# A mixture-of-experts stage cut into tiles of 256 slots instead of 512

## The reference

```python
x = x + _L0_gnn_ref(_layernorm(x), ...)        # 6 steps of a graph network on 3125 nodes, D = 256
x = x + _L0_ffn_ref(_layernorm(x)[None], ...)[0]

def _L0_ffn_ref(x, Wg, bg, bias, W1, b1, W2, b2):   # 8 experts, top 2, 256 -> 512 -> 256, float32
    gate_logits = x_flat @ Wg + bg + bias
    topk_vals, topk_idx = jax.lax.top_k(gate_logits, TOP_K)
    topk_w = jax.nn.softmax(topk_vals, axis=-1)
    h = jax.nn.relu(jnp.einsum('td,edh->teh', x_flat, W1) + b1)
    y = jnp.einsum('teh,ehd->ted', h, W2) + b2
    out = jnp.einsum('ted,te->td', y, combine)
```

## Time and profile before

| | |
|---|---|
| median of 3 runs | 2399.18 us |
| the profiled execution | 2399.45 us, its span 2397.7 us |
| mean granted clock of TensorE | 0.933 of 2.4 GHz |
| TensorE busy over the span | 84% |
| VectorE, ScalarE, GpSimd busy | 48%, 23%, 7% |
| expert stage | from 2087.5 us (first load issued) to 2320.4 us (last store landed) |
| tiles in it | 17, from one eviction to the same one of the next tile 12.7 us |

### The profile page before, as it was taken

How to read it: one execution, slowest core, us unless ns; L and a number is a source line. 1 busy time by engine, 2 the same in 40 slices (tenths; PEclk the granted TensorE clock), 3 DMA queues, 4 the chain that set the end, 5 groups by cost and what they waited for, 6 DMA issues and landing times.

```text
span 2397.7 us, 30332 instructions
## 1 busy us (share of the span) xinstructions
PE 2013.7 (84%) x11085; PEld 1418.0 (59%) x11086; DVE 1157.5 (48%) x2353; ACT 545.4 (23%) x1164; POOL 158.5 (7%) x228
## 2 busy tenths in 40 slices
PE   1766669999999999999999999999999952099960
PEld 1522236568756785578556865678567941088850
DVE  7599971345333452445233533444234565166643
ACT  0245541112211121112111221112112213132310
POOL 1011110000000000000000000000000003500026
PEclk7789999999999999999999999999999966599985
DMA  9500000000000000000000000000000114522224
GB/s 292 179 1 0 0 1 1 1 1 1 2 1 1 1 2 1 1 1 1 2 1 1 1 2 1 1 1 2 1 1 1 55 56 146 169 92 78 81 88 134
DMA packets 77945, 83.61 MB, mean 35 GB/s; under 512 B 10236, under 2 KB 72639, under 8 KB 77812
## 3 DMA queue, kind: packets, MB, share of 16 engines
q1 hardware_dynamic: 72244, 68.96, 9.1%
q0 software_dynamic: 5568, 12.82, 1.7%
HBM read 37.94 MB, written 43.81 MB: 34 GB/s over the span
## 4 chain that ended last, share of the span: by engine, by line
PE 76%; DVE 9%; issue 5%; POOL 4%; DMA 4%; SPq 1%; ACT 1%; DVEq 0%; POOLq 0%; ACTq 0%
PE bank L1236 33%; PE bank L1258 26%; PE bank L1223 5%; PE bank L1399 4%; DVE hot_key L668 4%; DMA slot_x<-slot_in 3%; PE bank L1162 3%; POOL slot_in L460 2%; POOL y_pair L470 2%; PE bank L1218 1%; PE bank L1311 1%; PE bank L1366 1%; DVE hot_row L662 1%; PE bank L1134 1%; PE bank L1331 1%
## 5 line engine op out<-in xcount | busy, mean ns | idle before, releaser
L1236 PE MATMUL bank<-adj,r_hi 128*128 128x512 fp8e4 (+2 forms) x2100 | 730.0, 352 | 0.0
L1236 PE MATMUL bank<-adj,r_lo 128*128 128x512 fp8e4 (+2 forms) x2100 | 729.2, 352 | 0.0
L1236 PEld LDWEIGHTS bank<-adj,r_hi 128*128 128x128 f16 x2100 | 205.3, 98 | 199.8 <-issue 16.3
L1236 PEld LDWEIGHTS bank<-adj,r_lo 128*128 128x128 f16 x2100 | 205.7, 98 | 183.5
L718 DVE TENSOR_TENSOR m_lo<-bank,m_hi 128x512 fp32r<-128x512 f32 (+2 forms) x84 | 49.5, 619 | 420.9 <-ACT m_hi L977 420.9
L1162 PE MATMUL bank<-hot_key,hot_row 128*128 128x400 f16 x588 | 140.0, 352 | 78.7 <-DVE hot_key L668 76.1
L1258 PE MATMUL bank<-x_hi,wht_hi 128*128 128x512 f32 (+2 forms) x504 | 195.1, 387 | 0.0
L1258 PE MATMUL bank<-m_hi,wct_lo 128*128 128x512 f32 (+2 forms) x504 | 184.9, 367 | 0.0
L1258 PE MATMUL bank<-m_hi,wct_hi 128*128 128x512 f32 (+2 forms) x504 | 184.6, 366 | 0.0
L1258 PE MATMUL bank<-x_lo,wht_hi 128*128 128x512 f32 (+2 forms) x504 | 184.4, 366 | 0.0
L1258 PE MATMUL bank<-m_lo,wct_hi 128*128 128x512 f32 (+2 forms) x504 | 184.3, 366 | 0.0
(11 more groups left out here) (278 smaller groups left out, 3300.2 us busy)
## 6 DMA issues: line engine op xcount, KB each, us to landing
slot_in<-zero_rows SPq DMA_DIRECT2D x1, 10752.0 KB, 37.5
slot_out<-zero_rows SPq DMA_DIRECT2D x1, 10752.0 KB, 68.1
slot_x<-slot_in SPq DMA_DIRECT2D x18, 512.0 KB, 4.0
slot_out<-slot_y SPq DMA_DIRECT2D x17, 512.0 KB, 3.2
raw<-in_L_ffn_W SPq DMA_DIRECT2D x32, 256.0 KB
x_scratch<-x SPq DMA_DIRECT2D x1, 3200.0 KB, 11.1
x<-x_scratch SPq DMA_DIRECT2D x1, 3200.0 KB, 13.3
xa<-in_x SPq DMA_DIRECT2D x1, 3072.0 KB
```

What stands on the lines that cost most here:

```text
L1236: last = mm(bank[2 * (w % 2) + f][:, 0:n], r[:, q, f * P:(f + 1) * P], c, start=q == 0 and i == 0, stop=q == NT - 1 and i == len(todo) - 1)
```

## The change

TILE becomes 256. A tile has 2 row blocks instead of 4, so everything that is 512 slots wide becomes 256 wide, and the output of a tile (2 x 256 columns) fills one bank, evicted once. The number of output banks per tile, YB, is 1, and the counts of the semaphores follow. With the numbers above the experts have 5, 11, 2, 1, 2, 5, 2 and 1 tiles, 29 in all. `slot_in` and `slot_out` get (32 + 1) x 256 = 8448 rows.

```diff
-TILE = 512
+TILE = 256
 TT = TILE // P
+YB = TT // 2
...
-                sp.wait_ge(sem("y_ready"), 2 * t + 4)
+                sp.wait_ge(sem("y_ready"), YB * t + 2 * YB)
...
-                    v.tensor_tensor(xt_lo[:, f, :], bank[4 + f][:], xt_hi[:, f, :].bitcast(F32), ALU.subtract).then_inc(sem("xt_split"), 1)
+                    v.tensor_tensor(xt_lo[:, f, :], bank[4 + f][:, 0:TILE], xt_hi[:, f, :].bitcast(F32), ALU.subtract).then_inc(sem("xt_split"), 1)
...
-                            v.tensor_scalar(act_h[h % 2][:], bank[h][:], hid_bias[:, i:i + 1], 0.0, ALU.add, ALU.max).then_inc(sem("h_relu"), 1)
+                            v.tensor_scalar(act_h[h % 2][:], bank[h][:, 0:TILE], hid_bias[:, i:i + 1], 0.0, ALU.add, ALU.max).then_inc(sem("h_relu"), 1)
...
-                        for j in range(2):
-                            dve.wait_ge(sem("y_sums"), 2 * n + (j + 3))
+                        for j in range(YB):
+                            dve.wait_ge(sem("y_sums"), YB * n + (j + 1 + YB))
...
-                    last = a.activation(xt_hi[:, f, :], bank[4 + f][:], ACT.Copy)
+                    last = a.activation(xt_hi[:, f, :], bank[4 + f][:, 0:TILE], ACT.Copy)
...
-                        act.wait_ge(sem("y_sums"), 2 * n + 2)
+                        act.wait_ge(sem("y_sums"), YB * n + YB)
...
-                            a.activation(h_hi[:, h, :], bank[h][:], ACT.Relu, bias=hid_bias[:, i:i + 1]).then_inc(sem("h_hi"), 1)
+                            a.activation(h_hi[:, h, :], bank[h][:, 0:TILE], ACT.Relu, bias=hid_bias[:, i:i + 1]).then_inc(sem("h_hi"), 1)
...
-            for name, n in (("h_lo", HT), ("y_sums", 2), ("y_ready", 2), ("y_stored", 1)):
+            for name, n in (("h_lo", HT), ("y_sums", YB), ("y_ready", YB), ("y_stored", 1)):
...
-                                    last = mm(bank[h][:], ws[:, t, e, h * P:(h + 1) * P], xs[:, t, :], start=k == 0, stop=k == 5)
+                                    last = mm(bank[h][:, 0:TILE], ws[:, t, e, h * P:(h + 1) * P], xs[:, t, :], start=k == 0, stop=k == 5)
...
-                        pe.wait_ge(sem("y_ready"), 2 * n + 2)
+                        pe.wait_ge(sem("y_ready"), YB * n + YB)
```

## The result

The kernel with tiles of 256 slots takes 2434.61 us (median of 4 runs, 2430.21 to 2442.19), the kernel before, on the same chip, 2399.02 us (2397.32 to 2400.26). The ratio is 1.0152 [1.0125, 1.0179]: slower by 35.6 us, where the forecast was +19. The profiled execution took 2433.20 us against 2399.45, +33.75 us.

A forecast was written before the change was run, and what follows sets the result against it. TensorE and the load's DMA, within 0.4 us of each other, were taken to bound the expert stage. Steady part +27.0, start -7.3, end -0.7 and zero fill 0 gave +19.0 us, 2418 us; range 2402 to 2442 us.

The forecast's parts named there:

- The ring of the load: Expert stage, per tile: eviction, store and load issue, load, transposes, output, next eviction; 12.72 us before, 8.24 us forecast.
- VectorE's blocks come next: Expert stage: if the load came a lot faster, VectorE's four blocks, 0.9 us each, would be next.
- Term A: From a tile's last eviction through store issue to load issue: independent of tile size, 1.79 us.
- Term B: From load issue to first transpose, 256 KB instead of 512: 3.0 us, own range 2.7 to 3.3 us.
- Term C: Transposes and output of a tile: 4 transposes and 24 output matmuls, half of before plus 0.03 us, 3.45 us.
- late load that I added: Steady part: one load slower than the others, as in the earlier trace; took 230.7 us to 231.8 us.
- Steady ring: First tile's last eviction to last tile's: 28 periods of 8.24 us, with one slow load 231.8 against 204.8 us, +27.0 us.
- The clock: TensorE's granted clock in the expert stage: stays at 1.00, so nothing for it in the sum.
- rival 1: TensorE idles 2 us per tile and its clock falls; half the tiles lose 1.3 us, 18 us: 2436 us; chance 0.25.
- Start: First tiles: a shorter first product hides less of the second load; first eviction at 2104.4 instead of 2111.71, -7.3 us.
- End: From the last eviction to GpSimd: the last store has 256 KB less, -0.7 us.
- Zero fill: Zeros written at the kernel's start, 4.7 MB less in all: no wait is for them, 0, within 1 us.

The follow-up runs named there:

- early load at 512 slots: The kernel before (tiles of 512), each load issued once `slot_x` is read, ahead of the wait for the eviction: 2398.72 us, ratio 0.9996.
- the early load: Each load issued once `slot_x` is read, ahead of the wait for the eviction; in the changed kernel (tiles of 256): 2381.85 us, ratio 0.9924.
- The two fills: The changed kernel with 14 or 7 extra matmuls per tile between first product and transposes, results unread: 2416.89 us and 2417.87 us.
- each alone: The kernel before with the load issued once `slot_x` is read: 0.9996; the kernel before with the output's block 3 last: 0.9994.
- both together: The kernel before (tiles of 512) with the load issued once `slot_x` is read and the output's block 3 last: 2389.29 us, ratio 0.9954.

## Why the prediction was right and wrong, by its own steps

- **What bounds the kernel.** The ring of the load is real, but it was half of the answer. The other ring, through the fourth block's `h_lo`, was not in the text, which said that the vector work is off the path. The experiment with the early load at 512 slots shows it as binding at 12.73 us, the load's ring being 12.67. For this change the omission cost nothing: at 256 the load's ring was well the longer one. It would have cost the whole gain had I proposed the early load for the kernel before. My remark that VectorE's blocks come next if the load came a lot faster holds: 6.86 us with the early load.
- **Term A**, 1.79 us: measured 1.78 and 1.79.
- **Term B**, taken as 3.0 us: measured 2.82, inside 2.7 to 3.3. The working was poorer than the value. I took the bytes at the rate near the end of one load, 389 GB/s, 0.68 us for 256 KB, where the difference of two whole loads is 1.28 us. And the earlier trace rows don't show that "a load starts slowly": at the 168 GB/s the store of 512 KB, issued at 2151.78, is still under way, and the DMA engines are as busy (0.97) as in the first 0.3 us after the load's issue, when what moves at 348 GB/s can hardly be the load's:

```profile
2152.75:2153.00 0.25, 0.25 (x2) 0.20 (x2) 0.00 (x0) 0.24 (x1) 0.00 (x0) 1.00 1.01 348
```

  A row of the DMA engines counts all transfers, so it gives no rate of one load while a store is under way. That 3.0 us came out near the measured value is in part luck: the allowance for the store's tail, 0.4 us, stood in for a slope that was too small by half. The row of 2.85 us of another tensor was the best single guide. By the Trainium skill's fit ("DMA: Bandwidth & Descriptors", section "Anatomy of one DMA") the load would take 2.6 us, and 0.3 us per 128 KB; the runs here, on another issue path, show 2.82 us and about twice that slope.
- **Term C**, 3.45 us: measured 0.66 + 2.86 and the latencies between them, some 3.6 us. The four transposes take more than half of the eight's 1.09. That is 0.15 us more, against 0.2 less in B, and the ring comes to 8.15 us for my 8.24; the late load that I added did not come either. Steady ring: +23.4 us for +27.0.
- **The clock: the step that failed.** I wrote "the granted clock 1.00 in the stage" and gave 0.75 to that. Nine of 28 tiles lost it. The measured mechanism is that of rival 1: 14 tiles x 1.3 us = 18 us and 2436 us there, 9 x 1.62 = 14.6 us and 2434.6 us here. That the totals are 1.4 us apart is partly luck: the count was too high and the price of a tile too low, and the steady ring's 3.6 us too much cancel the start's 3.0 us too little. The two fills, which leave the ring as it is, come to 2416.9 and 2417.9 us, so that the part of the clock is 16.7 to 17.7 us between medians; the nine tiles and the first tile's 1.5 us make 16.1 of it in the profiled execution. My evidence against it was one gap of 1.25 us at full clock, and the change makes gaps of 1.84 us in each tile: the row said nothing of that length, repeated every 8 us. Rival 1 was priced about right and given too small a chance. The Trainium skill ("TensorE: Matmul & The Clock Gate", section "HAM oscillation — how this bites in real kernels") has the clock lost on every tile where the compute is shorter than the DMA wait. I set it aside because here the wait is the shorter one. The trace shows the same loss, in a third of the tiles, with 6.3 us of compute to 1.84 us of wait: its direction was right here, and my use of its condition as a limit was not.
- **Start**, -7.3 us: measured -4.3. From the first transpose of the second tile to the eviction it took 5.1 us instead of 3.45, since the first output ran with the clock down:

```profile
2092.53 9.66 DMA slot_x<-slot_in
2102.24 0.66 PE bank L1367 x4
2102.91 4.38 PE bank L1400 x24
2107.38 0.70 DVE slot_y L907
```

  The clock makes 1.5 us of that. The second load landed at 2102.2 instead of the 2101.0 that I took, and 0.9 of these 1.2 us are there because the first load was issued at 2088.40, 0.9 us later than before. That part is no work of the change that I could name: over the kernels of this study the issue of that load lies between 2087.5 and 2091.3 us, though the expert stage and the size of the zero fill are all that was edited.
- **End**, -0.7 us: measured -0.4. **Zero fill**, 0: no effect seen, within a few us.

So the direction, the ring and its 29 turns were right. The time lies inside the range of 2402 to 2442 us because that was drawn to take in rival 1; it lies outside the forecast's own bounds, 2410 to 2427 us. The size was missed by one term, the clock, put at 0 in the sum and measured at 14.6 us in the steady part: a loss that I had as an alternative to the forecast, and that came on top of it.

## What to carry to other kernels

Write down the ring that sets a period with its fixed and its size-dependent terms: a smaller tile halves only the latter, and all the fixed ones are paid more often. Then look for every other ring of about the same length, because an edit of one of two rings of about equal length measures as nothing (0.9996 and 0.9994 here, each alone) and both together as a gain (0.9954). And where an edit lets TensorE stand idle in each period, add the price of the clock to the forecast instead of keeping it as a case beside it; here both work to fill the gap and another order of two DMA issues kept the clock up, and only the second shortened the ring as well.

## What was not expected of the hardware

TensorE's clock went down behind idle gaps of 1.83 to 2.02 us that came once in 8.15 us, and only in 9 of 28 tiles that look alike: the gaps of the other 19 are 1.67 to 1.95 us. In each of the nine the clock fell 0.1 to 1.5 us after TensorE had begun again. With gaps of 0.9 to 1.4 us (7 filling matmuls), 1.0 to 1.35 us (load ahead of the store) and 1.1 to 1.3 us (half the load) it fell in no steady tile. What picks the nine stays open. The experiments changed the length of the gap and TensorE's busy share together, so they don't say which of the two counts.
